# Two unused tensors, 32 and 224 bytes wide, ahead of the expert weights and ahead of the expert activations

## What is computed

```python
x = x + tanh(g_xattn[0]) * xattn(layernorm(x), ctx_768, Wq, bq, Wkv, bkv, Wo, bo)
# 16 heads, 77 context rows of 96 features a sequence
x = x + tanh(g_ffn[0]) * ffn(layernorm(x), Wg, bg, W1, b1, W2, b2)

# ffn: B, S, H, F, E, R, TOPK = (4, 256, 128, 512, 4, 4, 2)
cur = x
for r in range(R):
    flat = cur.reshape(-1, h)
    logits = flat @ Wg[r] + bg[r]
    vals, idx = top_k(logits, TOPK)
    w = softmax(vals, axis=-1)
    cw = sum(one_hot(idx, E) * w[..., None], axis=1)
    hmid = gelu(einsum('nh,ehf->enf', flat, W1) + b1[:, None, :])
    y = einsum('enf,efh->enh', hmid, W2) + b2[:, None, :]
    cur = cur + einsum('ne,enh->nh', cw, y)
```

## Time and profile before

| what | value |
|---|---|
| median of 3 runs | 463.22 us (463.19 to 463.77) |
| the profiled execution: its time | 463.65 us |
| the profiled execution: its span | 461.9 us |
| TensorE busy (PE) | 452.0 us, 98% of the span |
| weight loads (PEld) | 355.4 us |
| VectorE, ScalarE busy | 364.3 us, 359.9 us |
| GpSimd busy (POOL) | 70.0 us |
| TensorE's granted clock | full speed in all 40 slices |

### The profile page before, as it was taken

How to read it: one execution, slowest core, us unless ns; L and a number is a source line. 1 busy time by engine, 2 the same in 40 slices (tenths; PEclk the granted TensorE clock), 3 DMA queues, 4 the chain that set the end, 5 groups by cost and what they waited for, 6 DMA issues and landing times.

```text
span 461.9 us, 8784 instructions
## 1 busy us (share of the span) xinstructions
PE 452.0 (98%) x2856; PEld 355.4 (77%) x2856; DVE 364.3 (79%) x729; ACT 359.9 (78%) x742; POOL 70.0 (15%) x109
## 2 busy tenths in 40 slices
PE   8999999899999999999999999999999999999996
PEld 6666677678787888788878887888788878888885
DVE  6988989888878688768876887688768876887776
ACT  4777877696969779877987798778877887787873
POOL 6939884313000000000000000000000000000000
PEclk9999999999999999999999999999999999999999
DMA  6690000140020101300220022003100310023001
GB/s 163 191 202 17 1 9 11 32 154 3 0 92 24 70 2 43 143 0 1 67 118 1 1 87 99 0 2 113 72 0 0 141 45 1 0 80 128 24 0 45
DMA packets 12892, 25.18 MB, mean 55 GB/s; under 512 B 4615, under 2 KB 8496, under 8 KB 10800
## 3 DMA queue, kind: packets, MB, share of 16 engines
q1 hardware_dynamic: 9408, 22.23, 14.1%
q0 software_dynamic: 2784, 2.18, 2.6%
q10 hardware_dynamic: 656, 0.23, 0.2%
HBM read 22.82 MB, written 1.18 MB: 52 GB/s over the span
## 4 chain that ended last, share of the span: by engine, by line
PE 89%; DVE 6%; issue 2%; ACT 1%; DMA 1%; SPq 0%; POOL 0%; DVEq 0%; POOLq 0%
PE ps L1408 13%; PE ps L1410 13%; PE ps L1409 13%; PE ps L1395 12%; PE ps L1397 12%; PE ps L1396 12%; PE ps L1275 3%; PE ps L1297 2%; PE ps L1261 2%; PE ps L1303 2%; DVE least L897 1%; DVE rT_sb L913 1%; DMA x_sb<-in_x_dram 1%; PE ps L1310 1%; PE ps L1362 1%
## 5 line engine op out<-in xcount | busy, mean ns | idle before, releaser
L948 DVE TENSOR_TENSOR h_lo<-g_sb,h_hi 128x512 fp32r<-128x512 f32 x256 | 170.1, 688 | 76.0 <-ACT h_hi L813 76.0
L806 ACT ACTIVATE g_sb<-ps,cols 128x512 f32<-128x512 f32 x256 | 174.1, 691 | 41.4 <-PE ps L1397 40.8
L813 ACT ACTIVATE h_hi<-g_sb 128x512 fp32r<-128x512 f32 x256 | 155.5, 638 | 0.0
L1408 PE MATMUL ps<-h_hi,w_hi 128*128 128x512 f32 x252 | 102.4, 406 | 0.1
L1395 PE MATMUL ps<-x_hi,w_hi 128*128 128x512 f32 x256 | 101.0, 395 | 0.0
L1397 PE MATMUL ps<-x_hi,w_lo 128*128 128x512 f32 x256 | 100.1, 391 | 0.0
L1396 PE MATMUL ps<-x_lo,w_hi 128*128 128x512 f32 x256 | 99.8, 390 | 0.0
L1410 PE MATMUL ps<-h_hi,w_lo 128*128 128x512 f32 x252 | 99.6, 395 | 0.0
L1409 PE MATMUL ps<-h_lo,w_hi 128*128 128x512 f32 x252 | 99.4, 394 | 0.0
L1408 PEld LDWEIGHTS ps<-h_hi,w_hi 128*128 128x128 f32 x252 | 47.3, 188 | 14.0 <-issue 2.7
L1397 PEld LDWEIGHTS ps<-x_hi,w_lo 128*128 128x128 f32 x256 | 48.0, 188 | 11.4
(11 more groups left out here) (126 smaller groups left out, 394.9 us busy)
## 6 DMA issues: line engine op xcount, KB each, us to landing
cwb_even<-cw_rows SPq DMA_DIRECT2D x8, 1024.0 KB, 5.5
cwb_odd<-cw_rows SPq DMA_DIRECT2D x8, 1024.0 KB, 4.9
w_hi<-in_L_ffn_W_dram POOLq DMA_DIRECT2D x2, 1024.0 KB, 10.4
w_in<-in_L_ffn_W_dram SPq DMA_DIRECT2D x1, 1024.0 KB, 5.6
x_sb<-in_x_dram SPq DMA_DIRECT2D x3, 256.0 KB, 5.1
out_dram<-xn SPq DMA_DIRECT2D x3, 256.0 KB, 2.5
ctxT<-in_ctx_dram SPq DMA_DIRECT2D x3, 115.5 KB, 4.7
v_st<-v_sb SPq DMA_DIRECT2D x14, 19.2 KB
```

The lines of the kernel that those rows point to most:

```text
L806: nc.scalar.activation(g_sb[:, k, :], ps[:, k, :], ACT.Gelu_apprx_tanh, bias=b1_c[:, e * NF + k:e * NF + k + 1]).then_inc(gelu_done, 1)
L813: nc.scalar.activation(h_hi[:, u % 2, k, :], g_sb[:, k, :], ACT.Copy).then_inc(hi_done, 1)
L948: nc.vector.tensor_tensor(h_lo[:, u % 2, k, :], g_sb[:, k, :], h_hi[:, u % 2, k, :].bitcast(F32), ALU.subtract).then_inc(lo_done, 1)
L1408: mm(yb, w2_hi[:, w], hh, start=k == 0, stop=False)
```

## The change

Two tensors are declared that nothing reads or writes. `pad_weights` takes 32 bytes of each partition ahead of `w1_hi`, so everything behind it moves up by 32 bytes. `pad_routes` takes 224 bytes ahead of `cwb_even`, so everything behind that one moves by 256 in all. No instruction is added, removed, moved or resized: the lists of instructions of each engine of the two programs are the same.

```diff
@@ -110,6 +110,7 @@
         wg_w = sb("wg_w", [P, ROUNDS, 32])
         lgs = sb("lgs", [P, 2, P])
+        pad_weights = sb("pad_weights", [P, 8])
         w1_hi = sb("w1_hi", [P, E * F], F32R)
         w1_lo = sb("w1_lo", [P, E * F], F32R)
         w2_hi = sb("w2_hi", [P, E * NF * D], F32R)
@@ -145,6 +146,7 @@
         cw = sb("cw", [P, 2, E, TC])
         cwT = sb("cwT", [TP * E, P])
+        pad_routes = sb("pad_routes", [P, 56])
         cwb_even = sb("cwb_even", [P, 2, E, CH])
```

## The result

| what | before | after |
|---|---|---|
| median | 463.21 us | 457.54 us (4 runs, 457.26 to 457.99) |
| ratio of the fast runs | | 0.9873, 95% interval 0.9861 to 0.9886 |
| profiled execution: time, span | 463.65, 461.9 us | 457.99, 456.2 us |
| TensorE busy | 452.0 us | 445.0 us |
| a plain unit (no small piece, 24 matmuls) | 5.56 us | 5.44 us |

The change makes the kernel 1.3% faster, 5.9 us by the ratio. First the page after, answering to the earlier trace rows: span, busy time of the engines, and TensorE's groups of the expert products (busy us, mean ns of one). All lines stand two further down than before.

A forecast was written before the change was run, and what follows sets the result against it. The prediction took TensorE to bound the kernel, busy 452.0 of 461.9 us. Plain units' 7.56 us less 0.84, 0.2 and 0.28 left 6.24, so 463.22 - 6.24 = 457.0 us, range 455.4 to 463.4.

The forecast's parts named there:

- The pair of operands: Expert matmuls: distance modulo 256 between moving operand and weights sets the pace, 0.2267 us at 0, about 0.2333 at 32.
- The other engines and PSUM: Expert stage: two other explanations of down's slower pace, engine traffic and accumulation in PSUM, both argued against from the rows.
- A plain unit, 5.44 us: Expert stage: all 24 matmuls at 0.2267 us, 5.56 to 5.44, saving 0.12 a unit, 7.56 us over 63 units.
- half the gain: Rival: up's slow start stays, being due to place in the group; only down gains, 2.5 us, 460.7 us; chance 0.18.
- much faster: Rival: starting at multiples of 64 bytes removes part of the 32 extra cycles, 6.8 us more, 450.2 us; chance 0.05.
- Units with a small piece: 28 units with transposes or router logits: 0.84, 0.2 and 0.28 us not saved, leaving 6.24 of 7.56 us.
- The sum: Whole kernel: 6.24 us saved, giving 457.0 us against the median and a span of 455.7 us.
- Who becomes late: Expert stage: ScalarE's room shrinks from 0.64 to 0.52 us a unit; it stays ahead, so TensorE's gain is the kernel's.
- VectorE's own work: Expert stage: VectorE's two-input operations don't depend on the distance between their tensors (688 and 685 ns); no change.
- Attention and the end: Attention: nothing taken, since matmuls are short and the chain passes through VectorE and ScalarE; bound 1.2 us either way.
- ScalarE's wait: Sign of being right: ScalarE's wait for TensorE's up results shrinks from 40.8 to about 33 us.
- The Trainium skill's rule: Expert matmuls: independent read ports, so no address matters and time stays 463.2 us; kept within rival "no change", chance 0.14.

The follow-up runs named there:

- Experiments 1: Only the 32-byte pad ahead of the expert weights added to the kernel before (weights and x at 128, h at 160): 463.25 us, ratio 0.9995.
- Experiment 3: Mirror of the kernel before, made by three pads: weights and h at 128, x at 160, so distance 32 in up, 0 in down: 463.21 us, ratio 1.000.
- experiment 4: Against the changed kernel, w2 alone 32 bytes further (160), with w1, x and h still at 128 modulo 256: 461.36 us, ratio 0.9956.
- experiment 2: Only the 224-byte pad ahead of the routing weights added to the kernel before (weights, x and h all at 96): 457.26 us, ratio 0.9868.
- the map: Eight kernels with moving operands D bytes beyond the weights modulo 256 in both products, plus the changed kernel as D = 0: 457.54 to 467.00 us.
- D = 96: Against the changed kernel, x and h 96 bytes further with weights kept at 128, so distance 96 in both products: 465.76 us, ratio 1.0052.
- D = 224: Against the changed kernel, x and h 224 bytes further with weights kept at 128, so distance 224 in both products: 465.75 us, ratio 1.0050.
- D = 0: The changed kernel itself, weights, x and h all at 128 modulo 256, against the kernel before: 457.54 us, ratio 0.9873.

## Why the prediction was right, step by step

**What bounds the kernel.** Right. The expert stage was TensorE's throughout; 5.96 us of pace became 5.7 of span.

**The pair of operands.** Right, and this was the step that was a reading. Experiments 1 and 3 take the moving operand's place and the tensor `h` away as causes, experiment 4 shows that the weights' place counts as much, and experiment 2 that absolute alignment doesn't. The other engines and PSUM are out by experiment 4 too: nothing of theirs moved modulo 256 against the changed kernel, and `down` was slow again. For other distances than 0 and 32 the reading had nothing to say, and the map shows that these two don't give the rest.

**A plain unit, 5.44 us.** Right to the hundredth. The start of `up` lost its slow matmuls, which was the rival "half the gain": it was the `down` ahead, not slices 0 and 1. Experiment 3 shows it from the other side, where `down` behind a slow `up` starts slow. Of the rival "much faster" nothing showed: in no placement, weights at a multiple of 64 bytes included, does a plain unit take less than 5.44.

**Units with a small piece.** Forecast 0.03 of settling; measured 0.03 in the unit shown. `down` there went from 426.21 - 423.33 = 2.88 us to 2.83, a gain of 0.05 where 0.08 - 0.03 - 0.007 = 0.04 was in the sum. The start of the `up` behind it before the change:

```profile
426.21 0.40 PE L1395 MATMUL ps<-x_hi,w_hi 128*128 128x512 f32 x1
```

**The sum.** 6.24 us forecast, 5.96 measured in the stage. Read unit by unit from the traces, the 35 plain units gained 4.04 where 35 x 0.12 = 4.20 were priced: 5.56 us was taken for all of them, but they took 5.555 on average. The 28 with small pieces gained 1.92 where 6.24 - 4.20 = 2.04 was priced: unit 8 lost 0.21 to the longer wait for VectorE, and the others gained 0.09 more than their share. The errors are small and partly cancel. "Who becomes late" looked at ScalarE alone, with its mean room over all units. It was VectorE's routing weights in a single unit that became late, since a transpose waits for them there. That term was set at 0 and was 0.21. The price of nothing for VectorE's own work held: its subtraction and its addition take 688 and 685 ns after as before, though `cur` and `contrib` are now 0 and no longer 32 bytes apart modulo 256.

**Attention and the end.** Put at 0 within 1.2 either way; measured 0.18 + 0.08 worse. The start of `up(1)` isn't steady between the profiled executions: 93.75 us before, 93.93 after, 93.00 to 93.69 in the eight kernels of the map, and in experiment 2 it is this row's 92.92:

```profile
92.92 0.48 PE L1396 MATMUL ps<-x_hi,w_hi 128*128 128x512 f32 x1
```

Its stage is as short as the changed kernel's, 447.53 - 92.92 = 354.61 us, so the 1 us lies in attention. Whether addresses or the execution make it wasn't tried. The profiled execution after the change, 457.99 us, is the slowest of its four and experiment 2's, 456.86, the fastest of its four, and the medians are only 457.54 and 457.26, so most of it need not come from the addresses.

**ScalarE's wait** was forecast at about 33 us and came to 35.5. I took the whole 0.12 us off it in each of 64 units, 7.7 in all. TensorE's stage gained only 5.96, and ScalarE itself was busy 0.3 + 0.4 = 0.7 longer in its two groups. The page before:

```profile
L806 ACT ACTIVATE g_sb<-ps,cols 128x512 f32<-128x512 f32 x256 | 174.1, 691 | 41.4 <-PE ps L1397 40.8
L813 ACT ACTIVATE h_hi<-g_sb 128x512 fp32r<-128x512 f32 x256 | 155.5, 638 | 0.0
```

and after:

```profile
L808 ACT ACTIVATE g_sb<-ps,cols 128x512 f32<-128x512 f32 x256 | 174.4, 694 | 36.0 <-PE ps L1399 35.5
L815 ACT ACTIVATE h_hi<-g_sb 128x512 fp32r<-128x512 f32 x256 | 155.9, 640 | 0.0
```

5.96 - 0.7 = 5.3 us is what the wait lost. Why ScalarE's instructions took 2 to 3 ns longer wasn't tried.

**The Trainium skill's rule** ("TensorE: Matmul & The Clock Gate", Part 2: loading the next weights does not steal SBUF read bandwidth from the running matmul) doesn't hold for these operands, if it is taken to mean that no address matters. With the same instructions in the same order the pace goes from 5.44 to 5.63 us a unit with the distance between the two operands. Where the weights alone move (experiment 4) the matmuls follow each other more slowly, from the one on that runs while the moved weights are loaded. The loads are not recorded as longer: they take 188 ns on average on the page after, 187 or 188 on the page before. That SBUF's read bandwidth is what runs short isn't shown. The 215.8 ns that the prediction sets beside the paces is, on that page (Part 2, "Back-to-back issue gap"), the gap of an isolated matmul; no placement here settles below 226.7.

What stays open is the mechanism below that: which addresses clash and how, if clash they do. The map gives its outcome for nine distances with one ratio of lengths (512 bytes of weights against 2048 of moving operand), and the 32 cycles above 512 at the best distance weren't explained.

## What to carry to other kernels

This is shown for one shape in one kernel: float32r, 128x128 weights, 512 columns, a weight load for each matmul. If a stretch is bound by TensorE without gaps, compare the distance between starts of matmuls of one shape. Two paces for one shape, which neither the clock nor the other engines' work explains, point at where the weights and the moving operand lie relative to each other; a few bytes of padding decided it here, and an edit that adds or resizes a tensor ahead of one of them can win or lose 1 to 2% without touching an instruction. Put the two at the same address modulo 256 first, then measure.

## What the runs showed that was not expected

- The direction matters: with the moving operand 64 bytes further modulo 256 than the weights a plain unit takes 5.49 us, with it 64 bytes less far 5.60.
- A slow pace isn't one number. By the trace's nanoseconds the distances between starts repeat: 238, 231, 231 at D = 96, 235, 232 at D = 224, while at D = 0 each is 226 or 227.
- The pace has a memory. After a stretch at distance 32 the next matmuls at distance 0 need six or seven to reach 0.2267 us; after one at distance 224 the whole `up` group costs only 0.01 more than the fast 2.72. At distance 16 two paces hold over several units each in the same execution.
- Between the best and the worst placement of the same instructions lie 467.00 - 457.26 = 9.7 us, 2%.
